# A table of matrix products of constants ahead of fifteen waits of TensorE, in a four-block convolution and scan kernel

## Time and profile before

| | us |
|---|---|
| median of 3 runs | 1062.71 (1061.28 to 1067.70) |
| profiled execution, its time | 1064.98 |
| profiled execution, its span | 1062.8 |
| PE busy with matmuls | 922.9 (87%) |
| DVE busy | 734.4 (69%) |
| ACT busy | 550.9 (52%) |
| POOL busy | 355.4 (33%) |
| mean granted clock of PE | 0.927 |

### The profile page before, as it was taken

How to read it: one execution, slowest core, us unless ns; L and a number is a source line. 1 busy time by engine, 2 the same in 40 slices (tenths; PEclk the granted TensorE clock), 3 DMA queues, 4 the chain that set the end, 5 groups by cost and what they waited for, 6 DMA issues and landing times.

```text
span 1062.8 us, 19419 instructions
## 1 busy us (share of the span) xinstructions
PE 922.9 (87%) x7272; PEld 630.8 (59%) x7272; DVE 734.4 (69%) x2047; ACT 550.9 (52%) x1155; POOL 355.4 (33%) x320
## 2 busy tenths in 40 slices
PE   4687889999999999999999999999999998875843
PEld 2455556666766676666666666766676665544422
DVE  2566458687878787878788786878787868555332
ACT  1142453655657474747484755657474746361512
POOL 2012332425151615243342425151615242333100
PEclk9685979999999999999999998999999999896866
DMA  9101153252625353535444361625353534335060
GB/s 222 31 12 40 35 135 122 76 179 65 180 83 169 96 167 95 162 109 139 132 118 155 93 184 56 179 83 169 95 173 92 142 118 130 121 96 160 13 198 15
DMA packets 116545, 123.30 MB, mean 116 GB/s; under 512 B 64802, under 2 KB 99750, under 8 KB 116454
## 3 DMA queue, kind: packets, MB, share of 16 engines
q1 hardware_dynamic: 107812, 105.46, 34.2%
q0 software_dynamic: 6144, 13.71, 4.6%
q10 hardware_dynamic: 2498, 2.91, 1.2%
HBM read 84.32 MB, written 37.73 MB: 115 GB/s over the span
## 4 chain that ended last, share of the span: by engine, by line
PE 36%; DVE 28%; ACT 17%; issue 9%; POOL 4%; DMA 4%; SPq 1%; ACTq 1%; POOLq 0%; DVEq 0%
PE ps L620 33%; DVE c_w L1283 6%; ACT L968 3%; ACT d_pad L968 3%; ACT y L968 3%; DVE x L1291 2%; DVE b_xf L1291 2%; ACT x L968 2%; POOL b_res L1197 2%; DVE st L1318 2%; DVE y L1288 2%; DVE b_md L1283 2%; ACT c_hat L968 1%; SPq L1806 1%; DVE y L1291 1%
## 5 line engine op out<-in xcount | busy, mean ns | idle before, releaser
L1245 POOL DMA_INDIRECT b_yp<-y_turned,b_to x64 | 87.1, 1361 | 289.1 <-DMA y_turned<-b_yt 274.4
L620 PE MATMUL ps<-y,inw 128*128 128x392 f32 x384 | 138.2, 504 | 0.0
L1318 DVE BATCH_NORM_STATS2 st<-x 128x6 f32<-128x196 f32 x256 | 73.7, 352 | 88.9 <-POOL x L1197 76.6
L1197 POOL TENSOR_TENSOR rs<-ve,root 128x4 f32<-128x4 f32 x64 | 65.8, 1028 | 203.4 <-DVE ve L1287 202.9
L620 PE MATMUL ps<-c_w,c_zt 126*64 126x196 f32 x896 | 90.9, 352 | 23.6 <-DMA c_zt<-z_turned 10.6
L1283 DVE TENSOR_TENSOR c_w<-c_w,c_hat 126x1176 f32<-126x1176 f32 (+1 forms) x64 | 97.8, 1582 | 13.0 <-DMA c_w<-hat_turned 13.0
L620 PEld LDWEIGHTS ps<-y,inw 128*128 128x128 f32 x384 | 70.3, 193 | 42.3 <-issue 2.5
L620 PEld LDWEIGHTS ps<-c_w,c_zt 126*64 126x64 f32 x896 | 65.2, 145 | 44.5 <-issue 29.3
L620 PE MATMUL ps<-w,a_S 128*32 128x384 f32 (+2 forms) x1280 | 84.2, 403 | 6.3 <-DVE a_S L1291 6.3
L968 ACT ACT_TABLE_LOAD x50 | 64.2, 1283 | 38.3 <-PE ps L620 37.5
L1219 POOL DMA_INDIRECT x_turned<-b_xt,b_to x64 | 63.3, 989 | 34.7 <-DVE b_xt L1294 20.0
(11 more groups left out here) (203 smaller groups left out, 2092.2 us busy)
## 6 DMA issues: line engine op xcount, KB each, us to landing
c_w<-hat_turned SPq DMA_DIRECT2D x32, 771.8 KB
c_w<-hat_turned SPq DMA_DIRECT2D x32, 578.8 KB
z_turned<-c_z SPq DMA_DIRECT2D x32, 441.0 KB
c_zt<-z_turned SPq DMA_DIRECT2D x16, 882.0 KB
b_xp<-x_turned SPq DMA_DIRECT2D x32, 222.0 KB
x<-in_x SPq DMA_DIRECT2D x32, 196.0 KB, 2.7
y_turned<-b_yt SPq DMA_DIRECT2D x32, 196.0 KB
out<-x SPq DMA_DIRECT2D x32, 196.0 KB
```

The source lines that it names most:

```text
L620: return nc.tensor.matmul(o, l, r, start=start, stop=stop)
L1197: return nc.gpsimd.tensor_tensor(out=o, in0=x, in1=y, op=op)
L1245: nc.gpsimd.indirect_dma_start(out=YP[:, m, h].rearrange("p b d -> p (b d)"), out_offset=None, in_=y_dram[g % 2], in_offset=bass.IndirectO ...
L1318: last = nc.vector.bn_stats(st[s][:, 2 * c + b, :], x[:, c, b, :])
```

## The change

A table `BUSY` names fifteen fills, each by name and group, and a number for each. A new helper `take_early` takes the fill's bank, ahead of the wait for its data, and multiplies the identity by 256 columns of constants into it that many times. The real fill then starts with `start=True`, which overwrites these results. The five stages concerned call `take_early` ahead of their data waits and later fetch the same bank with `R.tile`. Fills and groups that the table does not name do no product; for them only the order of the two waits is turned round: bank first, data second.

```
+BUSY = {("n0", 1): 1, ("r3", 0): 1, ("w3", 0): 1, ("r1", 1): 5, ("n1", 0): 1, ("r1", 2): 6, ("n1", 1): 10, ("n2", 0): 7,
+        ("acc", 14): 12, (("pt", 0), 15): 6, (("pt", 1), 15): 6, ("acc", 15): 20, ("n3", 15): 7, ("d1", 15): 7,
+        ("d2", 15): 4}
...
+            def take_early(f, g, ring=R):
+                t = take(f, g, ring)
+                for _ in range(BUSY.get((f, g), 0)):
+                    mm(t[:, 0:256], ident, c128[:, 0:256])
...
+                    take_early(f"n{s}", g)
                     pe.wait_ge(stats[s].sem, stats[s].count(g))
-                    t = take(f"n{s}", g)
+                    t = R.tile(f"n{s}", g)
...
                 if i == 2:
                     if part == 0:
-                        take("acc", g, H)
+                        take_early("acc", g, H)
                         pe.wait_ge(c_w_ok.sem, c_w_ok.count(g, G))
                         pe.wait_ge(*z_in.at(g))
...
                 if i == 2:
+                    take_early("d2", g)
                     drained(pe, "d1", g)
-                    t = take("d2", g)
+                    t = R.tile("d2", g)
```

More of the change, by code:

```diff
@@ L673, in c0 @@
                 if i == 1:
+                    take_early("r1", g)
                     pe.wait_ge(a_md_ok.sem, a_md_ok.count(g))
@@ L676, in c0 @@
                         pe.wait_ge(prep, 1)
-                    t = take("r1", g)
+                    t = R.tile("r1", g)
                     for e in range(2):
@@ L721, in c0 @@
                 if i == 10:
+                    take_early("r3", g)
                     pe.wait_ge(a_m3_ok.sem, a_m3_ok.count(g))
-                    t = take("r3", g)
+                    t = R.tile("r3", g)
                     for e in range(2):
@@ L727, in c0 @@
                 if i == 11:
+                    take_early("w3", g)
                     pe.wait_ge(a_S_ok.sem, a_S_ok.count(g, 3))
@@ L730, in c0 @@
                         pe.wait_ge(ld_w[2], 16 * E4 * CC)
-                    t = take("w3", g)
+                    t = R.tile("w3", g)
                     for e in range(2):
@@ L837, in o1 @@
                     h = part
+                    take_early(("pt", h), g)
                     pe.wait_ge(*y_back[h].at(g))
-                    t = take(("pt", h), g)
+                    t = R.tile(("pt", h), g)
                     for b in range(G):
@@ L916, in k3 @@
                         pe.wait_ge(folded, 1)
-                    t = take("d1", g)
+                    take_early("d1", g)
+                    t = R.tile("d1", g)
                     conv1x1(t, lambda b, c: d1w[:, c, :], Y[3], 3, g).then_inc(R.filled("d1", g), 1)
                 if i == 2:
+                    take_early("d2", g)
                     drained(pe, "d1", g)
-                    t = take("d2", g)
+                    t = R.tile("d2", g)
                     conv3x3(t, lambda b, j: d2w[:, j, :], d_pad).then_inc(R.filled("d2", g), 1)
```

## The result

The changed kernel takes **1050.1 us** (median of 8 runs, 1048.38 to 1055.49) against 1062.01 us of the kernel before, measured beside it: ratio **0.9893**, 95% interval 0.9863 to 0.9923. Measured again, the ratio was 0.9861 (0.9811 to 0.9911).

What follows compares the result with a forecast made beforehand. PE was taken as slow and often idle at both ends, in chains of latency. Terms 1 to 3 (3.1), 4 (0.4) and 6 (2.5) sum to 6.0 us off the median 1062.71: forecast 1057, range 1051.5 to 1062.

Steps and rivals of the forecast that it cites:

- term 1: 37 to 82 us: `r3` and `w3` products keep the clock up through `a3`, 0.8 us less; about 0.6 survive.
- term 2: 78 to 102 us: `n1` to `d3` gains 1.4 us at full clock; `d3` to `yt` gains nothing, with 2.9 possible.
- term 3: `n2` of group 0: seven products keep the clock up through `c1`; together 1.5 us gained.
- term 4: `acc` of group 14 to `out` of group 15: 0.4 us from `pt`; the `out` gain only in the range.
- term 5: `acc` of group 15: its first part gets faster, then PE waits for DVE as before; gain nothing.
- term 6: Last block D: `n3` 0.2, `d1` 0.3 and `d2` 2.0 us faster, all 2.5 us counting.
- A: Clock holds wherever PE is not idle, so `d3` to `yt` and `out` run at full: 10.8 us, 1052; chance 0.18.
- C: Clock stays at half through the products ahead of `r1` of group 2 and `n1` of group 1: slower, 1066; chance 0.07.
- B: Products at the start too few to change any level there; the end alone gives 2.9 us, 1060; chance 0.22.
- D: The change does nothing, as gains at both ends only move waits for DMAs: 1062.7; chance 0.06.

Runs made afterwards that it cites:

- whole head: Only the table's first eight entries, up to `n2` of group 0, added to the kernel before; alone, ratio 0.9948 to that kernel.
- the sixteen products alone: Only the six products ahead of `r1` of group 2 and ten ahead of `n1` of group 1, against the kernel before: ratio 0.9974.

## Why the prediction was wrong, step by step

With four profiles of before and three of the change the difference of the mean spans, 1057.4 - 1047.1 = 10.3 us, can be split by landmarks of TensorE's list (start of one to start of the next, us, means; gains are taken before rounding):

| stretch | before | change | gain | forecast |
|---|---|---|---|---|
| start to `d3`, group 0 | 91.9 | 91.1 | 0.8 | 1.6 (term 1, `n1` to `d3`) |
| `d3` to `yt`, group 0 | 15.7 | 13.0 | 2.7 | 0 (term 2) |
| `yt` to `c1`, group 0 | 29.0 | 28.8 | 0.1 | 1.5 (term 3) |
| `c1` to the 14th `yt` | 709.3 | 710.0 | -0.6 | 0 |
| 14th `yt` to `acc` of group 14 | 123.3 | 121.7 | 1.6 | 0 |
| `acc` of group 14 to `c1` of group 15 | 22.9 | 21.5 | 1.4 | 0.4 (term 4) |
| to the last `acc`'s second part | 35.2 | 34.2 | 1.1 | 0 (term 5) |
| to the last `d1` | 13.5 | 12.6 | 0.9 | 0.2 (term 6, `n3`) |
| `d1` to the end | 16.6 | 14.3 | 2.3 | 2.3 (term 6, `d1` and `d2`) |

The long middle stretch (`c1` to the 14th `yt`) varies by 7.4 us within the four profiles of before, so the -0.6 there says nothing.

**The step that failed** is the choice in term 2: "I take the nearest row, that of one group later, which has the same list: the clock falls, gain nothing." That row was one draw of a place where the fall comes and goes, in the kernel before too; and it was not the right place. At the first `d3` the clock was low (0.50) in all four profiles of before, from 75 to 78 us on, and held (1.00) in all three of the change. 2.7 us of the 4.3 that the sum fell short are there. The bound that I had worked out and put aside, 2.9 us, was nearly the value. Over all runs, `d3` to `yt` of group 0 was 13.0 us in each of the eight profiles with the whole head. Of the ten without it nine had 15.3 to 19.2 us and one 12.5: in the kernel with `acc` and `pt` alone the clock was at half here too, but came back just ahead of `d3`, at 92 us. So the products make the full level here the rule, and it can come without them.

**Term 4** failed in the same way: the busy share of that row was carried over to `out`, and 0.4 us taken. `out` took 4.57, 4.82, 4.54 and 4.40 us in the four profiles of before and 2.90 in the three of the change; 1.4 us were gained over the stretch. Over all runs `out` took 2.87 to 2.90 us in the nine profiles with the entries of `acc` and `pt`, and 4.00 to 4.88 in the nine without: this cause is shown.

**Term 3** came out as its rows say only where the clock held. In the second profile of the change `yt` to `c1` was 27.5 us, 1.5 less than before, exactly the term. In the two others a new fall stands just ahead, at `out` of group 0; the change's first profile:

```profile
121.73 4.59 PE L623 MATMUL ps<-b_res,outw 128*128 128x392 f32 x8 [0.99 <-POOL b_res L1214]
...
126.16 3.19 PE L623 MATMUL ps<-c 128*128 128x256 f32 x14
...
132.26 1.88 ACT L985 ACTIVATE y<-x,gs,rs 128x196 f32<-128x196 f32 x4 [2.99 <-DVE gs L1308]
133.73 1.57 PE L623 MATMUL ps<-y,c1w 128*64 128x196 f32 x8
```

Before, that `out` took 2.90 us in all four profiles. So most of this gain was lost to a fall that had not been there: 0.1 us of the 1.5 were left. Why it comes here in two of three executions stays open.

**Term 1 and `n1` to `d3`.** The latter was 4.53 and became 2.94 us, gain 1.6 for a forecast of 1.4. `a3` ran at full (0.94 us), as said, but started later: 40.9 us in the mean where it was 39.9. One cause is seen: the product of `n0` of group 1, which I put at 0.4 us at half, took 1.22 us at half in all three profiles, with no idle time left behind it:

```profile
32.09 1.22 PE L623 MATMUL ps<-c 128*128 128x256 f32 x2
33.10 0.45 PE L623 MATMUL ps<-st,c 128*128 128x16 f32 x2
```

Of the gain 0.8 us remained. So terms 1 to 3 sum to 3.7 us, near the forecast's 3.1, but made up otherwise: that the sum came near is luck.

**Term 6** was right in mechanism and size. From `d1` to the end it is 14.1 to 14.6 us in every kernel that has these products in these numbers, and 16.2 to 16.7 in every one without. Of the 0.9 us ahead of `d1`, 0.2 are `n3`'s; the rest comes from the second part of `acc` (4.2 to 4.6 us where it was 4.7 to 5.5), which I had not counted.

**Term 5** was put at nothing. The 1.1 us in its row hang on one profile of before (37.3 us, the three others 34.3 to 34.8, the change 33.6 to 34.9), so a gain there is not shown.

What is left, 1.6 us between the 14th `yt` and `acc`, lies where the table names nothing, and the values of single profiles overlap there (`yt` of group 15 to `acc` of group 14: 12.9, 9.7, 12.9, 9.6 before, 11.2, 9.6, 10.9 in the change). This part stays open.

**The rivals.** A (the clock holds wherever TensorE does not stand idle) is nearest in time, 1052, and named the two right places. Its condition is too simple: with the sixteen products alone and in the change TensorE had the same idle time at `n1` and `a1` (1.46 and 0.55 us, 1.45 and 0.55 us), and the clock fell in the one and held in the other. C did not come: the sixteen ran at full (the ten in 4.56 us). B fell with the head's own 0.9948, D with the result.

**The range** was too narrow for a reason that could be seen: the kernel before varied by 6.4 us in three runs, and I read every row of one execution as its value. The profile I had, 1062.8 us, is the longest of four; the shortest is 1052.2. The gain, 1.07%, lies at the bound from which I called it faster, to which I gave 0.13.

**The time at half.** By the mean clocks (2 x (1 - clock) x span, as the levels are 0.50 and 1.00) TensorE was at half for 155, 126, 154 and 146 us before and 52, 54 and 76 us in the change, so 85 us less. A product takes about half as long at full (0.70 us where it is 1.48), so if all of that time were TensorE's work on the chain, the gain would be 42 us, as an estimate; 10.3 were measured. The time at half counted so holds idle time too (in 77.9 to 101.8 us TensorE was busy for 15.77 of 23.90 us) and work behind which TensorE waits for other engines, so the estimate is too high.

## What to carry to other kernels

Here, filling waits with products of constants paid where the work behind the wait is on the chain and would run at half, and where the products ended before the data came: counts that fit gave 1%, twice the counts lost 1.2%, at the same mean clock (0.975 in both profiles). The price of half-clock time is read from the chain, by the stretch from one landmark to the next at either level (here `d3` to `yt`, 15.8 and 13.0 us), not from the clock's mean. And before a term is taken from one row about the clock, look whether another place with the same list in the same trace, or a second profile, has the same value; if there is only one, give both ends a chance instead of choosing.

## What the runs showed of the hardware that was not expected

- Where the clock falls differs from execution to execution of the same program. From `d3` to `yt` of the second group the same kernel had 13.0 or 15.8 us.
- The work and the waits just ahead do not settle whether the clock falls. With the sixteen products alone it fell at about 89 us (`a1` 1.57 us), in the change it did not (0.88 us), though TensorE's rows of the 25 us before are the same in both.
- The granted clock in the profile is not the pace of the engine at the start of a run. In the kernel before it stands at 1.00 for the first 25 us (columns: span, busy TensorE, weight loads, DVE, ACT, POOL, clock, DMA):

```profile
0.00:25.00 25.00, 9.48 (x68) 6.45 (x72) 7.44 (x38) 4.46 (x11) 7.87 (x16) 1.00 0.90 220
...
14.67 1.93 PE L620 MATMUL ps<-w,a_S 128*32 128x128 f32 x32 [2.17 <-DVE a_S L1291]
17.15 1.57 PE L620 MATMUL ps<-y,a_w 128*64 128x196 f32 x8 [0.55 <-DVE a_w L1294]
```

But `w1` and `a1` take 1.93 and 1.57 us there. At the granted half they take 1.94 and 1.57 us (from 89.42 and 91.90 us on in the same profile), and at the granted full 1.08 and 0.88 us (in the change, from 88.58 and 90.21 us on). So TensorE ran at half up to about 20 us, in the change too (1.94 and 1.57 us). The mean granted clock of 0.80 in the first 159.8 us leaves this time out; no term of the prediction's sum used it.
